# Moving the softmax normalisation to GpSimd, starting the maxima a tile earlier and reordering the load queue of a two-layer attention

## What is computed

```python
attn = jnp.einsum('bqd,bkd->bqk', q * scale, k)
# first layer only: attn += rel_h[..., :, None] + rel_w[..., None, :]
attn = jax.nn.softmax(attn, axis=-1)
out = jnp.einsum('bqk,bkd->bqd', attn, v)
```

## Time and profile before

| | us |
|---|---|
| runs of the kernel (three) | 1000.21, 1007.57 (median), 1009.1 |
| the profiled execution | 1002.1 |
| its span, first to last instruction | 1000.3 |
| mean granted TensorE clock | 0.945 of full speed |
| busy in the span: TensorE, VectorE, GpSimd, ScalarE | 879.1, 526.9, 457.2, 328.3 |

### The profile page before, as it was taken

How to read it: one execution, slowest core, us unless ns; L and a number is a source line. 1 busy time by engine, 2 the same in 40 slices (tenths; PEclk the granted TensorE clock), 3 DMA queues, 4 the chain that set the end, 5 groups by cost and what they waited for, 6 DMA issues and landing times.

```text
span 1000.3 us, 17750 instructions
## 1 busy us (share of the span) xinstructions
PE 879.1 (88%) x6029; PEld 641.9 (64%) x6030; DVE 526.9 (53%) x883; ACT 328.3 (33%) x582; POOL 457.2 (46%) x360
## 2 busy tenths in 40 slices
PE   4969899999998899999898978616999999999991
PEld 3457466566665444555454534516999999999991
DVE  4334767676776444878788772722233333233224
ACT  0212144554545222445454544201222322322230
POOL 0000076676778200346464665558076177077303
PEclk9989699999999999999999989957999999999996
DMA  9564723534424019335464571351356455455214
GB/s 291 109 147 150 271 76 87 130 104 110 127 84 154 11 32 231 92 84 176 127 206 126 195 241 37 125 185 49 115 179 219 145 174 197 167 181 176 87 32 141
DMA packets 74367, 139.23 MB, mean 139 GB/s; under 512 B 11000, under 2 KB 49080, under 8 KB 74320
## 3 DMA queue, kind: packets, MB, share of 16 engines
q1 hardware_dynamic: 62720, 120.42, 39.3%
q10 hardware_dynamic: 9552, 11.93, 3.6%
q0 software_dynamic: 2048, 6.29, 2.0%
HBM read 91.39 MB, written 43.55 MB: 135 GB/s over the span
## 4 chain that ended last, share of the span: by engine, by line
PE 43%; issue 8%; DVE 8%; POOL 6%; DMA 3%; ACT 1%; DVEq 0%; SPq 0%; POOLq 0%; ACTq 0%
PE ps L796 14%; PE ps L807 11%; DVE mhalf L891 4%; PE ps L628 4%; PE ps L585 3%; PE ps L603 3%; POOL qf L518 3%; PE ps L727 2%; PE ps L618 2%; POOL xs L547 1%; POOL gy L556 1%; PE ps L683 1%; DVE rec L901 1%; PE ps L778 1%; ACT prob L1074 1%
## 5 line engine op out<-in xcount | busy, mean ns | idle before, releaser
L891 DVE TENSOR_REDUCE mhalf<-ps 128x1 f32<-128x512 f32 x384 | 242.0, 679 | 95.6 <-PE ps L603 94.1
L1074 ACT ACTIVATE prob<-ps 128x1024 f32<-128x1024 f32 x192 | 190.5, 1026 | 186.7 <-PE ps L628 110.0
L518 POOL TENSOR_TENSOR qf<-qf,prob 128x1024 f32<-128x1024 f32 x84 | 206.1, 2453 | 18.2 <-POOL qf L518 8.1
L796 PE MATMUL ps<-xT,w 128*128 128x128 f32 x1440 | 166.8, 278 | 1.6 <-ACT xT L1146 1.4
L796 PEld LDWEIGHTS ps<-xT,w 128*128 128x128 f32 x1440 | 166.1, 194 | 2.1 <-issue 2.1
L603 PE MATMUL ps<-km,qm 96*128 96x512 f32 x384 | 145.3, 445 | 20.1 <-DVE mhalf L891 15.3
L618 PE MATMUL ps<-qa,ka 97*128 97x512 f32 x384 | 147.4, 426 | 8.6 <-DMA qa<-row 8.2
L1163 ACT ACTIVATE h_f<-ps,b1c 128x128 f32<-128x128 f32 x240 | 68.4, 368 | 215.6 <-PE ps L796 161.0
L603 PEld LDWEIGHTS ps<-km,qm 96*128 96x128 f32 x384 | 74.1, 194 | 71.5 <-DVE mhalf L891 51.9
L514 POOL TENSOR_TENSOR qf<-prob 128x1024 f32<-128x1024 f32 x24 | 57.1, 2379 | 134.7 <-ACT prob L1074 134.7
L628 PE MATMUL ps<-prob,va 128*32 128x256 f32 x1536 | 109.8, 393 | 0.0
(11 more groups left out here) (130 smaller groups left out, 874.5 us busy)
## 6 DMA issues: line engine op xcount, KB each, us to landing
w<-in_w SPq DMA_DIRECT2D x24, 768.0 KB, 7.4
w_raw<-in_w SPq DMA_DIRECT2D x24, 768.0 KB, 12.0
heads<-parts SPq DMA_DIRECT2D x56, 256.0 KB, 4.7
qa<-heads SPq DMA_DIRECT2D x24, 256.0 KB, 3.7
ka<-heads SPq DMA_DIRECT2D x24, 256.0 KB, 3.9
qb<-heads SPq DMA_DIRECT2D x12, 512.0 KB, 5.1
xs<-zero SPq DMA_DIRECT2D x8, 768.0 KB, 4.9
qm<-heads SPq DMA_DIRECT2D x12, 384.0 KB, 3.7
```

The costliest lines, as they stand in the source:

```text
L518: pool.tensor_tensor(acc[b], acc[b], prob[:, n % NP, :], ALU.add).then_inc(a_ok[L], 1)
L796: last = mm(ps[:, g, c % HG * P:(c % HG + 1) * P], w1[b][:, k, c * P:(c + 1) * P], xT[:, k, :], start=(k == 0), stop=(k == KT - 1))
L891: v.tensor_reduce(mhalf[:, b, qt, half:half + 1], max_bank(qt, half), AX.X, ALU.max).then_inc(mx_ok[L], 1)
L1074: act.activation(prob[:, s % NP, :], ps[:, 2 + 2 * (s % 2):4 + 2 * (s % 2), :].rearrange("p a b -> p (a b)"), ACT.Exp).then_inc(p_ok[L], 1)
```

## The change

`output` moves from VectorE to GpSimd, as a multiplication of the same shape. GpSimd does it for head `h - 1` right behind its last add of head `h`; for the last head behind the one before it. `AHEAD` becomes 6: the maxima of the next head end beside `s == 1` instead of 2, those of the head after it begin beside `s == 2`, and `turn_max`, `turned_max` and `place_max`, which are placed by `TT - AHEAD`, each move a tile earlier. Head 0 does two tiles beside `s == 0`. SyncE's round becomes `load_m(h + 1)`, the zero fills, `store(h - 3)`, `load_a(h)`.

```diff
-AHEAD = 5
+AHEAD = 6
-MAXIMA_FIRST = [[(1, 5)], [(1, 6)], [(1, 7)], [(2, 0)], [(2, 1)], [(2, 2)], [(2, 3)], [(2, 4)]]
+MAXIMA_FIRST = [[(1, 5), (1, 6)], [(1, 7)], [(2, 0)], [(2, 1)], [(2, 2)], [(2, 3)], [(2, 4)], [(2, 5)]]
@@ SyncE
-                store(0, 0, 0)
                 with sp.Fori(0, (NH - 4) // 4) as q:
                     for n in range(4):
                         h = q * 4 + n + 3
                         load_m(h + 1, n % 2)
-                        load_a(h, 1 - n % 2)
                         if L == 1:
...
-                        store(h - 2, 1 - n % 2, n + 1, q)
+                        store(h - 3, n % 2, n, q)
+                        load_a(h, 1 - n % 2)
+                store(NH - 4, 0, NH - 4)
                 load_a(NH - 1, 1)
@@ GpSimd
+                def output(h, b):
+                    pool.wait_ge(o_rc[L], 4 * (h + 1))
+                    wait(pool, st_o[L][b], 32 * (h - b))
+                    pool.sem_inc(pool_in, 1)
+                    pool.tensor_tensor(osb[b][:], vsb[:, 0, :], rec[:], ALU.mult).then_inc(o_ok[L], 1)
+
-                def add_tiles(h, b, last=False):
+                def add_tiles(h, b, first=False, last=False):
                     for n in range(1, ADDS[L] + 1):
...
+                        if n == ADDS[L] and not first:
+                            output(h - 1, 1 - b)
+                    if last:
+                        output(h, b)
-                add_tiles(0, 0)
+                add_tiles(0, 0, first=True)
@@ VectorE
-                def output(h, b):
-                    wait(v, st_o[L][b], 32 * (h - b))
-                    v.wait_ge(o_rc[L], 4 * (h + 1))
-                    v.tensor_tensor(osb[b][:], vsb[:, 0, :], rec[:], ALU.mult).then_inc(o_ok[L], 1)
-
                 def head(h, b, first=False, left=2):
...
-                        if s == 6 and not first:
-                            output(h - 1, 1 - b)
...
-                output(NH - 1, 1)
```

## The result

| | us |
|---|---|
| the kernel before, median of 20 runs (range) | 1003.2 (999.27 to 1013.7) |
| the changed kernel, median of 20 runs (range) | 993.85 (986.49 to 998.04) |
| ratio, with its 95% interval | 0.9894 (0.9873 to 0.9914) |
| the profiled execution of the changed kernel, its span | 994.94, 993.1 |
| busy in it: TensorE, VectorE, GpSimd, ScalarE | 882.5, 489.5, 474.0, 328.2 |

The kernel became faster by 1.06%, some 10.6 us (the medians alone differ by 9.4). The forecast was a step of 22.6 from the profiled execution, to 980. The sign was right and the range held the time, but over half of the expected gain is missing. Medians count every run; the ratios leave out the few that stand far above the others of the same kernel.

A forecast was written before the change was run, and what follows sets the result against it. Bound by TensorE in the first layer, by waits between engines in the second. Terms -18.9 - 1.8 + 1.0 - 1.0 + 0.6 - 2.5 = -22.6 from 1002.1 gave 979.5, forecast 980 us; 8-in-10 range 968 to 996.

The forecast's parts named there:

- What bounds the kernel: First layer: TensorE's own work; second: VectorE's multiplication waiting for GpSimd's add, passed to TensorE by the three-bank ring.
- The multiplication leaves VectorE: Second layer: nine pieces shrink by 1.57 us (-14.1) and three clock dips go (-4.8); together -18.9, heads of 15.1.
- The first layer's odd head: First layer: one head of 19.5 us against 17.7, with the same wait and a late `load_m`; both go, -1.8.
- -1.0 for bank waits: First layer, maxima six ahead: longer score pairs cover the two-bank waits; 0 to -2 us over the layer, -1.0 taken.
- GpSimd takes it: Multiplication about 0.65 us on GpSimd, free in steady heads; 0.5 us at the end of each layer, +1.0.
- Head 0's doubled tile: Start of each layer: two reductions of 0.61 us brought forward; 0 to +1.2 a layer, +0.6 for both.
- The last head: End of second layer: the maxima's row leaves earlier, before most weight loads; gain nothing to about 3.6 us, -2.5 taken.
- The queue: SyncE's new order: `load_m` can go nearly a head early, `load_a(h)` has slack 4 us; price nothing.
- The row late each head: Rival: the row's transfers beside zero fills delay every head; 1 us a head gives 989; chance 0.15.
- The dips stay: Rival: second-layer clock dips remain because of small bank waits; 4.8 us back, 985; chance 0.12.
- Loads behind the store: Rival: `load_a` reaches tile 0 too late in each head of both layers, TensorE waits; chance 0.05, near 1012.
- The wait only moves: Rival: maxima stay VectorE-bound, the wait moves to another pair of tiles; chance 0.10, at 996.

The follow-up runs named there:

- second trace: Both kernels profiled once more, neither edited: the changed kernel took 985.81 us, the kernel before 1007.33 us.
- the new prologue order: Changed kernel with load_m(3) put ahead of load_a(2) before the loop, in both layers: median 986.64 us, ratio 0.9843 to the kernel before.

## Why the prediction was right or wrong

**What bounds the kernel: right.** VectorE's multiplication waited for GpSimd's add, and the three-bank ring passed that to TensorE. Putting it back brings the 1.22-us wait back, and doing it on VectorE beside an idle GpSimd doesn't.

The Trainium skill, "SBUF — State Buffer" (section "🔬 SBUF: two separate sides"), says that VectorE and GpSimd share a port pair which whoever starts first holds for its whole instruction, and counts VectorE operations with two SBUF inputs among those that need it, against a GpSimd operation that reads SBUF. The traces agree in both directions: 2.17 against 0.426 us for VectorE's multiplication, 3.31 against 0.40 for GpSimd's copy.

**The multiplication leaves VectorE, -18.9: right, with its condition.** Steady second-layer heads are 15.06 (15.1 forecast), tiles 0 and 1 took 4.48 (4.49), and the clock is 1.00 from 449 us on, so the dips went with the wait. Alone, though, the move made the kernel 1.6% slower.

**The first layer's odd head, -1.8: right;** its 19.5 us are gone, and the second trace of before had three of them. The -1.0 for bank waits isn't there: steady heads are 17.57, as they were.

**GpSimd takes it, +1.0: about right.** It takes 0.73, not 0.65, costs nothing in steady heads, and 0.7 in the last interval of each layer (16.77 and 14.22, against 16.09 and 13.51 with the multiplication in VectorE's idle slot).

**Head 0's doubled tile, +0.6: mis-sized.** From TensorE's first score of head 0 to GpSimd's first add of head 1 the first traces have 23.87 us before and 25.94 after in the first layer, 18.50 and 19.89 in the second: 3.5 us together. I had priced two reductions, and not the tile's own matmuls, which run at 1.2 GHz in the first layer and keep the clock low for longer. Moving the tile away gave back the first layer's part; the medians of that kernel (984.75 and 985.6) are 1 to 2 us below the one with only the new prologue order.

**The last head, -2.5: right in kind, too small.** The last second-layer interval fell from 18.34 to 14.22 (18.14 to 15.30 in the second traces). TensorE's wait of 5.49 us for the row is gone, and with five ahead 4.68 of it is there again. The multiplication has its part in the interval too: with it back on VectorE the interval is 16.83.

**The queue, "price nothing": this is the step that failed.** I wrote that `load_m` "can go nearly a head early". That is true in the loop, where the diff changes the order. It is false for the first `load_m` behind `load_a(2)`, which the diff leaves where it was while `AHEAD` = 6 needs its data a tile earlier. I had worked out the slack of one steady head and never of the prologue's three lines, although each head's `load_a` has to wait for the scores two heads back. It cost 7.7 us in the first trace, 2.5 in the second and about 5 by the ratios.

**The rest.** From the first traces the step was forecast as -22.6 and is -7.2 in the spans, 15.4 short. Inside the attentions the waits for `km` are 7.7 of that and head 0 in the first layer about 1; the second layer, apart from its wait, won 2.4 more than forecast. The other 9.2 us lie ahead of (3.3), between (2.1) and behind the attentions (3.8). Of these 2.2 are the doubled tile again (1.15 ahead and 1.06 between), since the parts are cut at first adds. The second trace of the kernel before is longer by 2.3, 1.5 and 1.3 us there, so 5 is scatter of that one execution. Some 2 us are left. A low clock in the projection between the layers, a group of six matmuls in 2.9 to 3.1 us instead of 2.1, appears in that second trace as well as in the changed kernel's first. Whether the change costs anything more there stays open. By the ratios, which don't hang on single executions, the step is 10.6 us; with the prologue's order put right it is 15.8, and with the tile of head 0 moved as well 19 to 21, of the 22.6.

**The rivals.** The row late each head: not with six ahead, since TensorE has no wait for it in a steady head; with five and the new order it is just that, in every second head. The dips stay: not where I had put them, since the clock is 1.00 from 449 us on; new ones follow the new wait. By the rule of the Trainium skill, "TensorE: Matmul & The Clock Gate" (section "A second HAM failure mode: psum-queue depth-cycling"), the small bank waits could have kept the dips; the trace from 449 us on doesn't bear that out here: 42 such waits, of 0.4 us at most and 14.1 in all, are left on the weight loads of the maxima, and the clock stays at 1.00. Loads behind the store: no wait for `qa` or `ka` from `heads` on TensorE in a steady head. I had argued there that the zero fills stand behind the loads of their round; in the new round they stand ahead of `load_a`. The wait only moves: not in every head, but once per layer, and to SyncE's queue instead of VectorE. No rival of mine had that.

## What to carry to other kernels

When a change needs data earlier, work out the slack of each load by its own place in the queue, with the prologue and the last round as cases of their own; an order that is fixed in the loop can still be the old one ahead of it. Before an operation is moved to another engine, see what its time consists of: here 1.7 of 2.2 us were a wait for another engine, and a slot where that engine is idle did as well. And move what sits behind the moved operation with it, since its new finishing time sets the store and all loads queued behind that.

## What the hardware showed that I had not expected

- TensorE's wait for `km` was often followed by a granted clock of 0.50, and not always: in the changed kernel after waits of 2.33 and 1.06 us, but not after 1.50 and 0.53 in the second trace; with the multiplication back on VectorE after 2.42, not after 0.94; with the multiplication alone behind seven of the eight waits over 1 us, but not behind one of 2.06. So the length alone doesn't decide. The 2.33 us cost twice their own length; a single trace doesn't tell what such a wait costs.
- VectorE and GpSimd hold each other up in either order: a 0.40-us copy on GpSimd took 3.31 and a 2.4-us add 5.27 behind one VectorE addition, and that was in the kernel before as well, at another instruction. I had read its 2.2-us multiplication only from VectorE's side.
- The first layer's head 0 begins at 1.2 GHz, and how soon the clock rises went with the matmuls that stand there: 3.9 to 5.9 us after its start in the seven executions with one query tile of maxima beside tile 0, 8.9 to 9.6 in the six with two.
